# Moving the front's last remainders and pieces behind the first group's maxima, and taking the first shift rows and scores ahead of group two

## The reference, cut to what matters

```
x = x + attn(layernorm(x))
q = (xn @ wq).reshape(B, T, H, D)              # T = 2048, H = 16, D = 16
lat = xn @ w_down
k, v = lat @ wk_up, lat @ wv_up                # the same shape as q
q, k = apply_rope(q), apply_rope(k)            # pairs turned by cos and sin of the position
scores = einsum('bqhd,bkhd->bhqk', q, k) / sqrt(D)
pages = arange(T) // 64
scores = where(pages[None, :] <= pages[:, None], scores, finfo.min)
out = softmax(scores) @ v @ wo
```

## Time and profile before

| | |
|---|---|
| median of 3 runs | 823.99 us |
| the profiled execution, its own time | 824.24 us |
| its span | 822.5 us |
| PE busy | 755.3 us, 92% |
| DVE busy | 620.3 us, 75% |
| ACT busy | 427.4 us, 52% |
| POOL busy | 149.9 us, 18% |
| DMA moved | 47.32 MB, mean 58 GB/s |

### The profile page before, as it was taken

The page is one execution under the profiler, slowest core; times in us unless marked ns, Lnnn a source line. Parts: engine busy times, 40 slices in busy tenths (PEclk is TensorE's granted clock), DMA queues, the critical chain, the costliest instruction groups (busy, mean ns, idle before and its releaser), DMA issues. The chain is left out here.

```text
span 822.5 us, 12183 instructions
## 1 busy us (share of the span) xinstructions
PE 755.3 (92%) x4329; PEld 393.8 (48%) x4329; DVE 620.3 (75%) x1107; ACT 427.4 (52%) x879; POOL 149.9 (18%) x170
## 2 busy tenths in 40 slices
PE   8874887999999999999999998899868999999997
PEld 5431232333223333222333231287547888888886
DVE  4899687888998899999898760067614778778786
ACT  1552463676667776657777867822123333333353
POOL 2564000000000000000000000013141455555520
PEclk9986797999999999999999998999999999999999
DMA  7796321120000000000440000030001222222103
GB/s 209 207 266 202 87 76 39 33 59 27 1 2 2 1 2 2 1 2 0 158 142 1 2 0 2 3 110 1 0 1 41 80 81 80 80 80 80 40 1 103
DMA packets 27152, 47.32 MB, mean 58 GB/s; under 512 B 6112, under 2 KB 23008, under 8 KB 26336
## 3 DMA queue, kind: packets, MB, share of 16 engines
q1 hardware_dynamic: 25184, 43.94, 17.8%
q10 hardware_dynamic: 1920, 2.75, 1.2%
HBM read 38.16 MB, written 8.39 MB: 57 GB/s over the span
## 5 line engine op out<-in xcount | busy, mean ns | idle before, releaser
L486 DVE TENSOR_REDUCE part_max<-psum 128x1 f32<-128x512 f32 (+3 forms) x560 | 341.4, 669 | 55.0 <-PE psum L672 50.0
L591 ACT ACTIVATE probs<-psum 128x512 f32<-128x512 f32 (+3 forms) x640 | 293.7, 539 | 155.5 <-PE psum L697 154.5
L672 PE MATMUL psum<-k_stack,q_stack 96*128 96x512 bf16 (+4 forms) x640 | 214.9, 364 | 18.6 <-DVE psum L472 11.2
L697 PE MATMUL psum<-q_stack,k_stack 98*128 98x512 bf16 (+4 forms) x640 | 202.3, 357 | 13.1 <-DMA q_stack<-shift 11.3
L709 PE MATMUL psum<-probs,v_all 128*17 128x512 f32 (+3 forms) x1280 | 149.7, 540 | 0.3
L672 PEld LDWEIGHTS psum<-k_stack,q_stack 96*128 96x128 bf16 (+1 forms) x640 | 60.1, 99 | 171.9 <-DVE part_max L486 121.5
L697 PEld LDWEIGHTS psum<-q_stack,k_stack 98*128 98x128 bf16 (+1 forms) x640 | 60.9, 99 | 94.3 <-ACT probs L591 39.2
L1471 PE MATMUL psum<-ctx_part,qc_part 128*128 128x512 f32 (+1 forms) x384 | 84.7, 371 | 5.0 <-POOL qc_part L1253 4.1
L877 POOL MEMSET eps<- 128x4 f32 x1 | 0.1, 102 | 459.6 <-POOLq L273 459.6
L1545 PE MATMUL psum<-v_parts,p_part 128*128 128x512 f32 (+3 forms) x416 | 76.9, 341 | 0.0
L1471 PEld LDWEIGHTS psum<-ctx_part,qc_part 128*128 128x128 f32 x384 | 67.3, 192 | 18.9 <-issue 4.9
(11 more groups left out here) (140 smaller groups left out, 681.6 us busy)
## 6 DMA issues: line engine op xcount, KB each, us to landing
mask<-in_mask SPq DMA_DIRECT2D x16, 800.5 KB, 4.4
pieces<-k_stack SPq DMA_DIRECT2D x24, 256.0 KB, 5.0
q_stack<-pieces SPq DMA_DIRECT2D x24, 256.0 KB, 4.2
k_stack<-pieces SPq DMA_DIRECT2D x24, 256.0 KB, 4.7
x_sb<-in_x SPq DMA_DIRECT2D x4, 512.0 KB, 8.9
out<-x_sb SPq DMA_DIRECT2D x8, 256.0 KB, 2.2
q_stack<-in_ctxT SPq DMA_DIRECT2D x1, 1601.0 KB, 11.1
probs<-in_cos ACTq DMA_DIRECT2D x4, 256.0 KB
```

Of the source, the lines that this page charges most:

```text
L486: nc.vector.tensor_reduce(part_max[:, h:h + m, r, c:c + 1], src, axis=AX_X, op=ALU.max).then_inc(m_read, 1)
L591: nc.scalar.activation(probs[:, s % 2, h, col:BLK], s_bank[h][:, col:BLK], ACT.Exp, scale=ATTN_SCALE).then_inc(exp_done, 1)
L672: last = nc.tensor.matmul(out, q_stack[b][0:rows, g * G + h, r * P:(r + 1) * P], k_stack[c][0:rows, g * G + h, 0:keys], start=True, stop=True)
L697: nc.tensor.matmul(s_bank[h][:, col:BLK], k_stack[s // TPB][0:rows, g * G + h, (s % TPB) * P:(s % TPB + 1) * P], q_stack[b][0:rows, g * G ...
```

## The change

DVE no longer does the last block's `remainder` and `last_piece` ahead of the first part. It waits until its own products are written (their banks are reused), clears `o_bank`, and reduces group (0, 0). The first "turn" now stands right behind group (0, 0)'s units instead of three units into group (0, 1)'s. Behind that turn DVE does `remainder(3)`, then all of group (0, 1)'s maxima, then `last_piece(3)`. PE issues the first scores right behind the first turn, ahead of group (0, 1)'s units. ACT takes the exponentials of those scores ahead of the last four cuts. SP sends the first shift rows between piece 0 and pieces 1 and 2 of the last block, and so ahead of the wait for all pieces and of the extra rows.

```diff
@@ the order of the stream
-            stream.insert(len(stream) - len(units[b]) + TURN_LAG, ("turn", k - 1, 0))
+            stream.insert(len(stream) - len(units[b]) + (TURN_LAG if k > 1 else 0), ("turn", k - 1, 0))
...
+    before = list(entries_of(0, -1))
+    till_shift = [e[0] for e in before].index("turn") + 1
@@ SP
+            def send_shift(b, g):
+
+                sp.wait_ge(shift_done, index(b, g) * 2 + 2)
+                for n in range(SHIFT_ROWS):
+                    dst = q_stack[b][TERM_ROWS + n:TERM_ROWS + n + 1, g * G:(g + 1) * G, :]
+                    sp.dma_start(dst, shift[:, n, :]).then_inc(shift_sent, 16)
...
-            for tb in range(2, NB):
-                for n in range(3):
-                    send(tb, n)
+            for n in range(3):
+                send(2, n)
+            send(NB - 1, 0)
+            send_shift(0, 0)
+            for n in (1, 2):
+                send(NB - 1, n)
...
             for k, (b, g) in enumerate(order):
-                send_shift(b, g)
+                if k:
+                    send_shift(b, g)
@@ DVE
-                remainder(tb)
+                if tb < NB - 1:
+                    remainder(tb)
                 if tb + 2 < NB:
                     norm(tb + 2)
-            last_piece(NB - 1)
-
+            dve.wait_ge(prod_done, 8 * NB)
             nc.vector.memset(o_bank, 0.0).then_inc(o_cleared, 1)
...
-            maxima(entries_of(0, -1))
+            maxima(before[:till_shift])
+            remainder(NB - 1)
+            maxima(before[till_shift:])
+            last_piece(NB - 1)
@@ ACT
-                for u in range(4):
-                    cut(tb, 1, u)
+                if tb < NB - 1:
+                    for u in range(4):
+                        cut(tb, 1, u)
...
             step(0, 0, 0)
+            for u in range(4):
+                cut(NB - 1, 1, u)
```

More of the change, by code:

```diff
@@ L319, in _ @@
             late = [(b, n, (s,)) for b in range(2, NB) for n, s in ((0, 0), (0, 1), (1, 0), (1, 1), (2, 0), (2, 1))]
[L320 to L325, removed]
             def prefetch():
```

## The result

The changed kernel takes 833.47 us, the median of 4 runs (832.85 to 833.71), against 823.93 us for the kernel before (4 runs, 823.23 to 825.46): 1.0112 times as long, interval 1.0095 to 1.013. The forecast was 832.5 us, with a range of 828.0 to 835.5. Run again on another occasion the changed kernel took 834.72 us against 824.18, 1.0119 (1.009 to 1.0148).

A forecast was written before the change was run, and what follows sets the result against it. It took the chain from the seam through shift-row landings to the scores of (0, 1) as the bound. Hold 7.6 plus clock 0.7 made 8.3, added to 824.24: 832.5 us, range 828.0 to 835.5.

The forecast's parts named there:

- The first half: At the seam, clearing without the six subtractions ahead starts 6.7 us earlier, and the first scores 10 us earlier.
- DVE's last pieces come late: On DVE, the two last pieces take 2.62 us and end at 90.2, behind group (0, 1)'s maxima.
- The hold in the queue: On SP's queue, extra rows (10.1 us) and three loads (3.0) delay the second pair; scores of (0, 1) 7.6 us later.
- landing term: Before the scores of (0, 1), the time from the last shift packet to the scores: 0.4 us.
- high end: At the scores of (0, 1), 2.1 us in place of 0.4 after the extra rows: 9.3 us later.
- The clock: After PE's idle wait of some 10 us, a slower clock costs 0.7 us; bounds 0 and 1.8.
- one unit more in the first part is one less in the next: 0: On PE around group (0, 0), moving one unit between parts costs nothing: 0.
- What it moves by, the end moves by: The start of the scores of (0, 1), at 98.58, shifts the kernel's end by the same amount.
- rival C: Ahead of (1, 0), up to 3.7 us of the delay is swallowed by PE's 3.74 us idle: 828.8 us; chance 0.06.
- Rival A: On the slow DMA engines, the three loads don't add behind the extra rows: 829.5 us; chance 0.19.
- B: On SP's queue, the second pair of shift rows is not held up and lands in 2.33 us: 823.7; chance 0.12.
- D: At the kernel's end, the front's gain of 6.7 us arrives, so it is faster: 817.5 us; chance 0.04.

The follow-up runs named there:

- e10: The changed kernel run again unedited for a second profile: 834.72 us.
- e2: Changed kernel with the first three loads issued behind the second pair of shift rows, extra rows still ahead: 829.87 us.
- e6: Changed kernel with filler matmuls on PE while it waits for the second pair of shift rows: first 50 (835.09 us), then, the long one, 104 (834.04 us).
- e7: Kernel before with only the turn and first scores moved ahead of group (0, 1)'s units: 829.08 us.
- e1: Changed kernel with the extra rows issued behind the shift rows of group (0, 3): 825.96 us.
- e3: Changed kernel with the second pair of shift rows issued ahead of the wait for all pieces, the extra rows and the first loads: 832.13 us.
- e5: Changed kernel with the second pair of shift rows ahead of the wait for all pieces and the extra rows behind (0, 3)'s shift rows: 821.39 us.
- e4: Kernel before with the extra rows issued behind the shift rows of group (0, 3): 824.28 us.
- e9: Changed kernel with e5's edits and block 2's loads dealt 3, 3, 4, 2 instead of 3, 5, 2, 2: 820.51 us.
- e8: Changed kernel with each late six-row load of extra rows cut into six one-row loads: 839.98 us.

## Why the prediction was right

**The first half gained as worked out.** From the front's end, 67.44 in the profile before and 69.48 after, PE's first unit starts 0.72 us later (0.61 was forecast), the first scores 11.26 (11.36) and group (0, 1)'s units end with DVE's neg_max at 19.97 (20.06).

**DVE's last pieces come late: right, with one term too large.** The pieces were put at 2.62 us, as beside POOL in the kernel before; alone they took 1.28, and the remainders 2.50 instead of 3.65. So SP's second pair was issued 26.85 behind the front's end instead of 28.36: 1.5 us better than forecast. PE, too, was through with group (0, 0) 3 us sooner than forecast (94.96, which is 25.5 behind the front's end, instead of 28.6). That made its wait 13.28 us and not some 10, but did not move the scores, which the landing set.

**The hold in the queue: right in kind, one term too small.** The forecast was 106.15 - 95.8 = 10.35 us from issue to scores; it took 11.90, and 12.33 in e10. In e2 the extra rows drained in the 10 us that I took from the earlier trace rows (issued from 92.40, last traffic in the window 102 to 103), and the loads added 3.4 and not 3.0. The rest is the time from the last packets to the scores. From the issue of the extra rows to the scores it took 15.2 us where the sum had 10.1 + 3.0 + 0.4 = 13.5, so this landing term was 1.3 too small: 1.7 and not 0.4, near the 2.1 that I had kept for the high end. The error in the hold and the earlier issue cancel: 7.6 us were forecast for the scores of (0, 1), 7.6 came in the first profile and 8.4 in the second.

**The clock: mis-sized.** I took 0.7 us from group (0, 0) of the kernel before and 1.8 as the upper bound. Group (0, 1) took 2.1 and 3.0 us more; e6 shows that 1.7 and 2.6 of it are the clock, and e7 that the other 0.45 comes with the new order ("one unit more in the first part is one less in the next: 0" was not quite 0). The comparison was bad: group (0, 0) and (0, 1) don't hold the same work, so their difference isn't the price of a cold start.

**"What it moves by, the end moves by": not quite.** The waits of (0, 2) and (1, 0) moved rigidly with the rest, so rival C's mechanism (part of the 3.74 us given back) didn't happen. But the stretch of low clock behind the wait at (1, 0) was 14 us long in the kernel before and 8 in the changed one, on the same work; this gave back 1.8 us:

```profile
152.00:153.00 1.00, 1.00 (x4) 0.28 (x3) 1.00 (x3) 0.46 (x1) 0.00 (x0) 0.50 0.01 0
154.00:155.00 1.00, 0.79 (x7) 0.24 (x4) 1.00 (x3) 0.60 (x1) 0.00 (x0) 1.00 0.00 0
```

That is 7 us behind the scores of (1, 0) at 147.50, where the earlier trace rows show 0.53 still 12 us behind 135.72.

**How close the number is, is partly luck.** Against the forecast's parts the first profile has +2.0 by the front's spread, +1.4 in group (0, 1), -1.8 at (1, 0) and -0.9 behind it, which add up to less than 1 us. In the second it is -0.2, +0.8 at the seam, +2.3, -2.2 and +0.7. By the medians the loss was 9.5 and 10.5 us where 8.3 were forecast.

**Rival A** falls with e2. **Rivals B and D** fall with e1 to e3: the shift rows were held, for 8 to 9.5 us, and nothing of the front's gain could reach the end. What the rivals left out is that the front's gain is real and can be had: with no shift rows behind the extra rows (e5) the same change is 3.6 us faster than the kernel before, while moving the extra rows alone (e4) gains nothing that can be told.

## What to carry to other kernels

When work is moved behind a chain's next link, look at the queue of the engine that issues for both: here a wait for the moved work put 10 us of unurgent loads directly ahead of 8 KB that the whole core waits for. Here a small urgent transfer took the time of what was ahead of it on its DMA engines (2.35 us free, 11.9 behind both). So sort a shared queue by when its transfers are needed, and give slow loads a gap in which no urgent one is issued. And price an idle gap of TensorE with the slower clock behind it, measured on the same work (here 1.7 to 2.6 us behind some 13 us of idle time).

## What the runs showed of the hardware that I had not expected

The length of a stretch at 1.2 GHz varies on the same work. All kernels wait 3.73 to 3.75 us at (1, 0). At that wait and behind it the granted clock was below 0.9 in 14 one-us windows in the kernel before, e3, e4, e5, e9 and the long e6, in 11 in e1, in 7 or 8 in the changed kernel, e2, the first e6, e7 and e8, and in 4 in e10. From the shift rows of (1, 0) to those of (1, 1) it was 24.5 to 25.3, 23.9, 23.1 and 22.7 us. What sets the length is not shown. Times of single runs go with the mean granted clock: e1's ten runs lie between 822.90 us at 0.967 and 830.28 at 0.953.

DVE's subtraction of two tiles of 128x512 in SBUF takes 1.3 us while POOL does the like, and 0.64 when POOL is idle: 2.62 for two beside POOL's 2.97 in the kernel before, 1.28 alone at 89.36 in the changed one.

A one-row load of 16 KB costs SP 0.62 us to issue, a six-row one of 96 KB 0.34.
